# Gate logits and node table projected from the unnormalised residual with centred weights, and the sort's turns 13 half steps later, in a two-layer graph kernel

## The reference, cut to what matters

```
x = x + L0_gnn(layernorm(x), adj, ...)            # attention inside each graph
x = x + L0_ffn(layernorm(x), gate_w, gate_b, ...) # each node goes to one of 8 experts, with a capacity
x = x + L1_gnn(layernorm(x), adj, ...)            # attention inside each graph
x = x + L1_ffn(layernorm(x), W_gat, ..., edges)   # attention over 524288 edges, then 4 experts, top 2

L0_ffn: logits = layernorm(x) @ gate_w + gate_b ; idx = argmax ; prob = softmax(logits)[idx]
L1_ffn: h = layernorm(x) @ W_gat                  # the node table that the edges gather from
layernorm(x) = (x - mean) / sqrt(var + eps)       # no learned scale at these places
```

## Time and profile before

| what | us |
|---|---|
| median of 3 runs (lowest, highest) | 3086.28 (3086.01, 3090.51) |
| the profiled execution, own time | 3091.0 |
| its span, first to last instruction | 3088.6 |
| stage A, with its tail to the last `place` | 73 to 608.7 |
| first experts to the end of the sort (stage B) | 708.65 to 1251.6 |
| stage C, from the ranked edges on | 1288 to 1640.6 |
| stage D | 1640.6 to 3088.6 |
| busy: PE, DVE, ACT, POOL | 58%, 73%, 39%, 60% of the span |

### The profile page before, as it was taken

One profiled execution on the slowest core, in us unless ns is written; L12 is line 12 of the kernel. 1 busy time (PEld: TensorE's weight loads), 2 busy tenths in 40 slices (PEclk: granted clock), 3 DMA queues, 4 the chain that ended last, 5 costly groups with the idle time before them and its releaser, 6 DMA issues. The chain is left out here.

```text
span 3088.6 us, 31245 instructions
## 1 busy us (share of the span) xinstructions
PE 1796.8 (58%) x8829; PEld 1241.0 (40%) x8829; DVE 2253.5 (73%) x4422; ACT 1204.5 (39%) x2447; POOL 1843.8 (60%) x1723
## 2 busy tenths in 40 slices
PE   0676764308888888375874244565446554565445
PEld 0555653305555555265773122232223322333223
DVE  7999978698899999887754456555665556655566
ACT  2576674514444444065872122222222222222222
POOL 5600024773445444377676777777777777777772
PEclk9899885559999999588876677877777776777777
DMA  5697000110111110222111121222122211222111
GB/s 214 211 356 295 4 18 22 39 36 24 34 49 40 47 43 13 69 77 77 28 38 39 39 41 34 42 44 42 31 42 44 45 42 31 42 44 42 37 39 36
DMA packets 170130, 192.35 MB, mean 62 GB/s; under 512 B 59241, under 2 KB 126096, under 8 KB 169008
## 3 DMA queue, kind: packets, MB, share of 16 engines
q1 hardware_dynamic: 107616, 118.69, 11.5%
q0 software_dynamic: 57088, 62.48, 10.0%
q10 hardware_dynamic: 5328, 9.97, 0.9%
HBM read 91.70 MB, written 105.25 MB: 64 GB/s over the span
## 5 line engine op out<-in xcount | busy, mean ns | idle before, releaser
L1523 POOL DMA_INDIRECT edge_rows<-node_table,edge_ids x1024 | 996.8, 973 | 313.2 <-issue 296.5
L1148 POOL DMA_INDIRECT token_results<-arena,token_of x160 | 249.3, 1558 | 301.2 <-ACT arena L1084 221.3
L585 DVE TENSOR_TENSOR sort_ping<-sort_pong 128x1024 f32<-128x1024 f32 (+1 forms) x232 | 395.2, 1745 | 12.6 <-ACT sort_pong L1018 8.1
L1141 POOL DMA_INDIRECT slots<-arena,send x128 | 174.9, 1366 | 376.2 <-ACT arena L1040 340.8
L585 DVE TENSOR_TENSOR sort_pong<-sort_ping 128x1024 f32<-128x1024 f32 (+1 forms) x230 | 390.0, 1736 | 8.6 <-ACT sort_ping L1018 3.7
L1646 PE MATMUL x_b_featT<-ident,x_feat 128*128 128x128 f32 x128 | 34.8, 427 | 619.6 <-PEq L1245 619.6
L1393 DVE TENSOR_TENSOR win_score<-win,masked 128x320 f32<-128x320 f32 x64 | 28.7, 490 | 446.4 <-DMA win<-edge_table,win_ids 445.2
L1652 PE MATMUL x_b_hid<-x_featT,x_w 128*128 128x512 f32 x512 | 311.0, 762 | 28.3 <-PEq L1245 28.3
L1659 PEld LDWEIGHTS x_b_res<-x_w,x_hid 128*128 128x128 f32 x2048 | 246.8, 197 | 97.1 <-issue 97.1
L1646 PEld LDWEIGHTS x_b_featT<-ident,x_feat 128*128 128x128 f32 x128 | 22.9, 217 | 625.0 <-issue 625.0
L1659 PE MATMUL x_b_res<-x_w,x_hid 128*128 128x128 f32 x2048 | 271.8, 288 | 0.0
(11 more groups left out here) (348 smaller groups left out, 4214.8 us busy)
## 6 DMA issues: line engine op xcount, KB each, us to landing
edge_table<-zeros SPq DMA_DIRECT2D x8, 5120.0 KB, 35.7
edge_rows<-node_table,edge_ids POOLq DMA_INDIRECT x1024
arena<-slots SPq DMA_DIRECT2D x40, 260.0 KB, 2.6
slots<-zeros SPq DMA_DIRECT2D x2, 5120.0 KB, 24.4
edge_table<-edge_rows SPq DMA_DIRECT2D x64, 160.0 KB, 2.1
out_dram<-x_y ACTq DMA_DIRECT2D x33, 256.0 KB
x<-in_x_dram SPq DMA_DIRECT2D x4, 2048.0 KB, 16.2
adjacent<-in_adj_dram SPq DMA_DIRECT2D x32, 256.0 KB, 2.7
```

The lines of the kernel that those rows point to most:

```text
L585: step(dve.tensor_tensor(vb[:, :, t, :], va[:, :, 0, :], va[:, :, 1, :], op))
L1141: pool.indirect_dma_start(slots_dram, bass.IndirectOffsetOnAxis(send[:, q:q + 1], 0), sent_feat[:, n % 2, v, :], None, bounds_check=EXPERT ...
L1148: pool.indirect_dma_start(rows_dram, bass.IndirectOffsetOnAxis(token_of[:, n % 4, r:r + 1], 0), res[:, n % 2, r, :], None, bounds_check=TO ...
L1523: pool.indirect_dma_start(rows[:, u, c, :], None, table_dram, bass.IndirectOffsetOnAxis(ids[:, u, c:c + 1], 0)).then_inc(rows_in[u], 16)
```

## The change

Both projections take x as it is. With W centred over the features (its column means taken off), x @ W equals (x - mean) @ W, and the division by the standard deviation is done on the result. So `act_normalise` goes, for both; PE transposes x itself once it is updated; PE sums the weight's columns with a matmul of ones and DVE subtracts the means, once for each weight; the gate's logits get their scale and bias in `choose`, by two more instructions on 128x256 for each chunk; the table gets its scale a chunk of 8 groups at a time (`dve_scale`), and SP's transfer of that chunk waits for this. The gate's groups come 9 iterations earlier (`LEAD` = 3 for 12), so that the loop ends with n = 39 on DVE; `LAG` is 3 for 12. `Projection` has one bank for its product instead of two names for one, and its keep stands at n - LAG - 1; on ACT its copy stands ahead of the attention's step instead of behind it. In stage C the keeps behind the loop come in one piece, ahead of the searches. And every entry of `TURNS_AFTER` moves by 13 half steps, with half steps 80 to 83 behind the last expert.

```diff
 class Gate:
-    def act_normalise(self, act, g, rstd, shift):
-        act.wait_ge(self.norms[g // self.chunk].done, self.norms[g // self.chunk].turn + 1)
-        ge(act, self.turned, g - 1)
-        normalise(act, self.feat[:, g % 2, :, :], self.x, rstd, shift, g).then_inc(self.normed, 1)
     def pe_turn(self, pe, g):
-        pe.wait_ge(self.normed, g + 1)
+        pe.wait_ge(self.updated, g + 1)
         ge(pe, self.featT_s, g)
         for v in range(PER):
-            last = pe.transpose(self.b_featT[:, v, :], self.feat[:, g % 2, v, :], self.ident)
+            last = pe.transpose(self.b_featT[:, v, :], self.x[:, g * PER + v, :], self.ident)
     def dve_keep(self, dve, g):
-        dve.tensor_tensor(self.into[:, at:at + PER, :], self.b_out[:, :, :], self.bias.unsqueeze(1).to_broadcast([P, PER, EXPERTS]),
-                          ALU.add).then_inc(self.kept, 1)
+        dve.tensor_scalar(self.into[:, at:at + PER, :], self.b_out[:, :, :], 1.0, None, ALU.mult).then_inc(self.kept, 1)
 class Projection:
-                normalise(act, self.feat[:, u % 2, :, :], self.x, self.rstd, self.shift, f).then_inc(self.normed, 1)
     def pe_step(self, pe, n, u):
-            a = n + 1
+            a = n + 2
             if live(a):
-                pe.wait_ge(self.normed, a + 1)
-                ge(pe, self.featT_s, a - self.ahead + 1)
+                pe.wait_ge(self.updated, a + 1)
+                ge(pe, self.featT_s, a)
             if live(n):
                 pe.wait_ge(self.featT_s, n + 1)
-                ge(pe, self.kept, n - self.ahead + 1)
+                ge(pe, self.kept, n)
+    def dve_scale(self, dve, c, chunk, rstd):
+        part, each = self.into[:, c * chunk * PER:(c + 1) * chunk * PER, :], rstd.unsqueeze(2).to_broadcast([P, chunk * PER, self.cols])
+        dve.wait_ge(self.kept, (c + 1) * chunk)
+        dve.tensor_tensor(part, part, each, ALU.mult).then_inc(self.scaled, 1)
...
-        PROJECTED = {12 + g + g // GATED: g for g in range(GROUPS)}
-        LAST_OF = [12 + (c + 1) * GATED - 1 + c for c in range(CHUNKS)]
+        LEAD = 3
+        PROJECTED = {LEAD + g + g // GATED: g for g in range(GROUPS)}
+        LAST_OF = [LEAD + (c + 1) * GATED - 1 + c for c in range(CHUNKS)]
-        LAG, CHUNK = 12, GROUPS // 4
+        LAG, CHUNK = 3, GROUPS // 4
-        TURNS_AFTER = {-1: (0, 1, 2, 3), 8: (4,), 9: (5, 6, 7), 18: (8,), 19: (9, 10, 11), 28: (12,), 29: (13,), 30: (14,), 31: (15,),
+        TURNS_AFTER = {12: (0, 1, 2, 3), 21: (4,), 22: (5, 6, 7), 31: (8,), 32: (9, 10, 11), 41: (12,), 42: (13,), 43: (14,), 44: (15,), 53: (16,),
...
             def choose(c):
                 L = logits[:, :, :]
+                dve.wait_ge(x0_norms[c].done, c + 1)
+                link2(dve.tensor_tensor(L, L, wide(x0_norms[c].rstd), ALU.mult))
+                link2(dve.tensor_tensor(L, L, gate_b[:, :].unsqueeze(1).to_broadcast([P, ROWS, EXPERTS]), ALU.add))
...
             dve.wait_ge(gate_in, 32)
+            dve.wait_ge(gate_summed, 1)
+            dve.scalar_tensor_tensor(gate_w[:, :], b_centre_gate, -1.0 / FEAT, gate_w[:, :], ALU.mult, ALU.add).then_inc(gate_centred, 1)
...
-                if n >= LAG:
-                    gat.dve(dve, n - LAG)
+                gat.dve_keep(dve, n - LAG - 1)
+                if n > CHUNK and n % CHUNK == LAG:
+                    dve.wait_ge(gat_norms[n // CHUNK - 1].done, n // CHUNK)
+                    gat.dve_scale(dve, n // CHUNK - 1, CHUNK, gat_norms[n // CHUNK - 1].rstd)
...
-            for n in range(GROUPS + 1 - LAG, GROUPS):
-                gat.dve(dve, n)
-                if n % 3 == 0:
-                    search()
+            for n in range(GROUPS - LAG, GROUPS):
+                gat.dve_keep(dve, n)
+            dve.wait_ge(gat_norms[-1].done, GROUPS // CHUNK)
+            gat.dve_scale(dve, GROUPS // CHUNK - 1, CHUNK, gat_norms[-1].rstd)
...
-                sp.wait_ge(gat.kept, (c + 1) * CHUNK)
+                sp.wait_ge(gat.scaled, c + 1)
...
+            for half_step in range(2 * STEPS, max(TURNS_AFTER) + 1):
+                turns(half_step)
```

More of the change, by code:

```diff
@@ L313, with __init__ @@
 class Gate:
[L316 to L320, removed]
[L322 to L325 removed]
+    def __init__(self, sem, x, updated, chunk, ident, weight, featT, b_featT, b_out, into):
+        self.turned, self.featT_s, self.projected, self.kept = (sem(f"gate_{n}") for n in ("turned", "featT", "projected", "kept"))
+        self.x, self.updated, self.chunk, self.ident, self.weight, self.into = x, updated, chunk, ident, weight, into
+        self.featT, self.b_featT, self.b_out = featT, b_featT, b_out
     def pe_turn(self, pe, g):
[L328 removed]
+        pe.wait_ge(self.updated, g + 1)
         ge(pe, self.featT_s, g)
         for v in range(PER):
[L331 removed]
+            last = pe.transpose(self.b_featT[:, v, :], self.x[:, g * PER + v, :], self.ident)
         last.then_inc(self.turned, 1)
@@ L348, in dve_keep, with __init__, act_step @@
         at = g % self.chunk * PER
-        dve.tensor_tensor(self.into[:, at:at + PER, :], self.b_out[:, :, :], self.bias.unsqueeze(1).to_broadcast([P, PER, EXPERTS]),
-                          ALU.add).then_inc(self.kept, 1)
+        dve.tensor_scalar(self.into[:, at:at + PER, :], self.b_out[:, :, :], 1.0, None, ALU.mult).then_inc(self.kept, 1)
 class Projection:
[L354 to L358, removed]
-            sem(f"{tag}_{n}") for n in ("normed", "turned", "featT", "projected", "kept"))
-        self.x, self.rstd, self.shift, self.ident, self.weight, self.cols, self.into = x, rstd, shift, ident, weight, cols, into
-    def act_step(self, act, n, u):
-            a, f = n + 1, n + 2
+    def __init__(self, sem, tag, x, updated, ident, weight, cols, into, featT, b_featT, b_out):
+        self.turned, self.featT_s, self.projected, self.kept, self.scaled = (
+            sem(f"{tag}_{n}") for n in ("turned", "featT", "projected", "kept", "scaled"))
+        self.x, self.updated, self.ident, self.weight, self.cols, self.into = x, updated, ident, weight, cols, into
+        self.featT, self.b_featT, self.b_out = featT, b_featT, b_out
+    def act_step(self, act, a, u):
             if live(a):
@@ L929, in _ @@
             pe.wait_ge(gate_in, 32)
+            pe.matmul(b_centre_gate, ones[:, :], gate_w[:, :], start=True, stop=True).then_inc(gate_summed, 1)
             for n in range(-3, LAST_OF[-1] + 2):
@@ L1007, in _ @@
             pe.wait_ge(gat_made, 2)
+            pe.matmul(b_centre, ones[:, :], gat_w[:, :], start=True, stop=True).then_inc(gat_summed, 1)
+            pe.wait_ge(gat_made, 3)
             for n in range(-3, GROUPS + LAG):
                 att1.pe_step(pe, n, n % 4)
-                gat.pe_step(pe, n - LAG, n % 4)
+                gat.pe_step(pe, n - LAG, (n - LAG) % 4)
         @block.scalar
@@ L1047, in _ @@
                     x0_norms[n // GATED - 1].act_root(act)
-                if n + 2 in PROJECTED:
-                    if PROJECTED[n + 2] == 0:
-                        act.wait_ge(masked_s, GROUPS)
-                    gate.act_normalise(act, PROJECTED[n + 2], rstd, shift)
                 for c in range(CHUNKS):
```

33 lines of the change are left out of this document (21 added, 12 removed).

## The result

The changed kernel takes 3172.36 us (median of 4 runs, 3162.55 to 3175.46); the kernel before, 3086.15 beside it. The ratio is 1.0271, with a 95% interval of 1.0247 to 1.0295: 86 us slower. The forecast was 3116 with a range to 3140; the sign was right, the size was not.

A forecast was written before the change was run, and what follows sets the result against it. DVE's sort was taken to bound stages A and B, the PE-ACT-DVE round beside POOL's fetches stage C; sort's end +22 us (3 + 22 - 3) and stage C +8 on 3086.3 gave 3116 us, 3096 to 3135 by bounds, stated range 3080 to 3140.

The forecast's parts named there:

- Stage A: Window where DVE sorts while serving the attention; half its 28.2 us of waits for ACT go, added work 12 to 13.
- the `place`: DVE's `place` at n = 39, ending stage A's loop: 3 us later, bounds 10 earlier and 10 later.
- Stage B: Window where the sort's end on DVE, not the experts, releases stage C; sort ends 22 us later, bounds 10 to 33.
- the rival of short scatters: Last chunk's 32 scatters take 0.97 us, rows land 30 us earlier, total 3086; chance 0.13.
- turn 0: First turn on PE, behind `hidden(7)`: PE reaches it at 714, DVE ready at 661 waits 53 us.
- wait for DVE at turn 4: Sign in stage B that the forecast is right: PE waits for DVE at turn 4.
- Stage C: Window where PE, ACT and DVE hand iterations round beside POOL's fetches: 8 us longer, bounds -5 and +18.
- The ring: Stage C: PE's projection waits for DVE's same-iteration keep; 7.41 us a turn against 6.78, +9 us over 15 iterations.
- the ring's price in iterations with `combine`: Stage C: ring 8.91 us against old period 8.90; 0 to 15 us added, 4 taken.
- the rival "PE's clock falls in stage C": PE's waits in the new ring lower its clock; 15 late iterations grow by 30 us, total 3145; chance 0.08.
- the last search: End of stage C: POOL's last fetches, then one to three searches, end at 1634 to 1647 against 1638.
- the rival "stage C gains": Keep comes in time, POOL's 8.58 us wait and some 7 us go: -16 instead of +8, total 3092; chance 0.15.

The follow-up runs named there:

- The run with the old table: Changed kernel with the node table (`Projection`, `LAG` 12, bank, keeps, searches) of the kernel before, gate and turns as changed; 3116.7 us, ratio 1.0092.
- the idle matmuls: Changed kernel plus unused 128x96 matmuls on PE ahead of stage C's projection, 12 per iteration up to n = 16, then 6; 3136.9 us, ratio 1.0157.
- the keep ahead: Changed kernel with stage C's keep moved between DVE's scores and its copy of PE's last product; 3113.3 us, ratio 1.0082.
- the ring open: Changed kernel with the keep before DVE's copy: alone 3113.3 us, with idle matmuls 3117.7, with turns 3 half steps later 3053.3, with turns as before 3062.4.

## Why the prediction was right and wrong

**Stage A.** Sized a little short: the `place` came at +8.7 instead of +3, inside its bounds. I let half of DVE's waits for ACT go; 24.8 of 28.2 us stayed. The normalise of the gate left ACT's iterations (84 instructions of line 90), but the sends, now nine iterations earlier, came into them (32 more); that these are what kept the waits is likely, but no run shows it.

**Stage B.** Right in mechanism, and the sum came out within its bounds: the sort's end moved by 29.8 us against 22 (by 24 to 30 in the five runs that share stages A and B), with 10 to 33 as bounds. The scatters took their 2 us again, so the rival of short scatters fell, and DVE waited for PE at turn 0. But the 54.8 us beside a forecast of 53 are partly luck. DVE was ready for the first half of turn 0 at 669.6 instead of 661, and it did not wait from there: it still had the second half to sort, 9.6 us, which the prediction left out. PE came to turn 0 at 729.5 instead of 714, mostly because the rows came at 651 and not at 639. And the four turns took 17.2 us (729.53 to 746.69, at a granted clock of 1.00) instead of 21 to 22, a figure taken from a place where the clock was 0.81. One of the signs did not come: PE had no wait for DVE at turn 4 (790.15). The run with the old table tests the sum without stage C: 28 us against 22. The scatters next to wide sort steps took 1.85 to 2.03 us from the second of the last chunk to its end. What the Trainium skill says in "SBUF — State Buffer", "Who interferes with whom", of software DMAs that DVE holds up agrees with these rows only in part: the same section reports a probe in which `tensor_tensor`, which the sort steps are, did not stall DMAs. Here the scatters beside it took about twice the 0.97 us of the others, and the measurement decides.

**Stage C.** Here the prediction failed, and at a step that can be named. The ring was found, and its length in a plain iteration at full clock was nearly right: 7.41 us worked out, 7.63 and 7.62 measured; with `combine` 8.91 worked out, 9.13 measured. But at the clock that PE got, the late iterations took 8.38 on average, where 7.3 to 7.8 had been named as the sign. Two terms were wrong. First, the ring's price in iterations with `combine`: I set 8.91, a plain iteration, against 8.90, the mean of nine old ones, and took 4 us. That mean has iterations with the layer norm's steps in it, one with a pass of 2.28 us over the keys, and some that wait longer for PE, whose clock was 0.88; a plain old one took 7.86, from DVE's L279 of the one to that of the next:

```profile
1382.47 1.13 DVE L279 SCALAR_TENSOR_TENSOR x<-banks,att_small,x 128x128 f32<-128x128 f32 x4
...
1390.33 1.13 DVE L279 SCALAR_TENSOR_TENSOR x<-banks,att_small,x 128x128 f32<-128x128 f32 x4
```

So the ring added over 1 us to each plain iteration, and the norm's steps, which stand ahead of the keep, lengthen it further where they come. With the idle matmuls, at 0.98, the ten iterations took 9.82 us on average; with the keep ahead they took 8.78. The ring came to as much as 24 us instead of some 13. Second, and larger, the clock: the rival "PE's clock falls in stage C" had a chance of 0.08 and 30 us, and it is what happened, with 35. I argued against it from stage B, where PE has waits in every step and 0.95. That was the wrong neighbour: the tail of stage C, in the same, showed 0.50 with PE busy 25.71 of 41 us, and the loop to be forecast lies between the two. The page "TensorE: Matmul & The Clock Gate" of the Trainium skill, section "HAM oscillation — how this bites in real kernels", tells of loops whose waits throttle PE in every round, waits longer than most of those here (1.4 and 2.9 us in plain iterations, 5.1 at the longest). The trace agrees in kind (0.79 and 0.85 of full speed over the loop, back at 0.98 and 0.93 when the waits are filled), though not in every round: the iteration behind a wait of 1.38 us above ran as fast as one with the wait filled.

The two terms feed each other, which a sum of independent terms doesn't show: a longer ring means more waiting for PE, so a lower clock (0.79 and 0.85 with the ring, 0.88 and 0.91 without), so a longer ring (35 us).

**What ends stage C.** I took the last search. In the changed kernel that ended 8 us before stage D began, and in all seven runs with the new table POOL's first instruction of stage D came 11.27 us behind its last fetch. With the old table it was 11.42, 11.69 and 11.85, and 2 to 3.4 us behind the last search; what came last there is not shown. For the sum this changed little. It would have shown, though, that the rival "stage C gains" had little room: POOL's fetches and these 11.3 us take 331 of the 354.8 us, and the stage did not go below 348 in any run.

**The rivals.** Short scatters: excluded by the trace. Stage C gains: excluded with the ring closed; with the ring open the stage was 3 to 7 us shorter than before in three profiled executions, not 16. The falling clock: right, beside a ring that was dearer than taken.

**Slips in the working.** With its own bounds the sum gives 3091 to 3137, not 3096 to 3135. Between the `place` at 559 and 608.86 DVE was not waiting most of the time: it was busy for 30.3 of 49.7 us. A scatter at 682.04 beside the narrower sort steps took 1.96 us, so that 0.97 was not the rule there. And stage C of before ended 386.4 us behind the sort, not less than 385. None of these changes the 3116.

## What to carry to other kernels

When a change shortens the lag between two loops, list for each engine what its next instruction now waits for in the *same* iteration; a buffer that is free one iteration earlier or later decides whether engines overlap or form a ring, and moving one instruction of 0.25 us ahead in its engine's order was worth 59 us here. Where a ring contains TensorE, price it at both clocks and take the lower one as a real case, since the ring's own waits can bring it about. And when the start of a stage moves, place what is interleaved with it by when its own engine is ready for it, not by how far the stage moved: 13 half steps followed the experts, while 3 fitted the sort.

## What the runs showed of the hardware that was not expected

Idle matmuls in place of waits made the kernel 35 us shorter: PE's granted clock over the loop went from 0.79 and 0.85 to 0.98 and 0.93. Where PE did not set the pace the same matmuls raised the clock as well (to 0.98 and 0.96) and brought nothing. The clock fell though PE's only waits between 1580 and 1618 were of 1.37 and 1.38 us: it was granted 1.00 from 1608.73 to 1616.36 and 0.55 from 1617.90 to 1621.20. POOL's scatters ran in step with DVE's wide sort steps: two of them with their gaps, 1.90 + 0.30 + 2.02 + 0.30 us, take as long as one step of two instructions, 4.53. And POOL's last indirect fetch is followed by 11.27 us until the next stage's first instruction on that engine in all seven runs with the new table, and by 11.42 to 11.85 in the three with the old one.
